# A gated cross-attention stack: weighing three scoring steps behind, with five buffers of exponentials

## The reference

```python
def attend(xn, ctx, l):                 # heads: 16 of 8 features (l = 0, 1, 3), 4 query heads of 32 with 1 key head (l = 2)
    q, k, v = heads(xn @ Wq), heads(ctx @ Wk), heads(ctx @ Wv)
    s = q @ k.T * scale                 # l = 0: + adj, masked; l = 1: rotary, causal; l = 2: rotary, masked by key
    return (softmax(s) @ v) @ Wo
x = x + tanh(g_xattn[0]) * attend(layernorm(x), ctx, 0)
x = x + tanh(g_ffn[0]) * route8(layernorm(x))            # the one of 8 matrices with the highest score, per token
x = x + tanh(g_xattn[1]) * attend(layernorm(x), ctx, 1)
x = x + tanh(g_ffn[1]) * top2_lora(layernorm(x))         # top 2 of 8 low-rank experts, relu
x = x + tanh(g_xattn[2]) * attend(layernorm(x), ctx, 2)
x = x + tanh(g_ffn[2]) * route8_gelu(layernorm(x))       # one of 8 experts of width 512, gelu, layer norm
x = x + tanh(g_xattn[3]) * attend(layernorm(x), ctx, 3)
x = x + tanh(g_ffn[3]) * moe(layernorm(x))               # not zero for the first two rows only
```

## Time and profile before

| what | us |
|---|---|
| median of three runs | 1077.09 |
| the profiled execution | 1068.41 |
| its span, first to last instruction | 1066.7 |
| PE busy | 880.5 |
| DVE busy | 787.8 |
| ACT busy | 493.7 |
| POOL busy | 302.4 |

### The profile page before, as it was taken

One profiled execution on the slowest core, in us unless ns is written; L12 is line 12 of the kernel. 1 busy time (PEld: TensorE's weight loads), 2 busy tenths in 40 slices (PEclk: granted clock), 3 DMA queues, 4 the chain that ended last, 5 costly groups with the idle time before them and its releaser, 6 DMA issues.

```text
span 1066.7 us, 19274 instructions
## 1 busy us (share of the span) xinstructions
PE 880.5 (83%) x7316; PEld 573.0 (54%) x7316; DVE 787.8 (74%) x1849; ACT 493.7 (46%) x753; POOL 302.4 (28%) x324
## 2 busy tenths in 40 slices
PE   1778787788899998887898877787888999998686
PEld 1533346454566676663465323564456667776443
DVE  3899998778666945449778999878779574554783
ACT  2655453345534532217874656234554343322475
POOL 3600246443443211100323023655335330110000
PEclk9999777698989999988999989677998999988899
DMA  9100000000000000000110000000000000000000
GB/s 322 33 2 2 2 1 1 1 2 2 2 1 2 2 1 6 6 1 2 42 32 21 2 2 1 1 1 2 3 3 1 1 2 1 1 1 1 2 7 17
DMA packets 11741, 14.26 MB, mean 13 GB/s; under 512 B 1604, under 2 KB 10716, under 8 KB 11396
## 3 DMA queue, kind: packets, MB, share of 16 engines
q1 hardware_dynamic: 11552, 12.88, 3.7%
q10 hardware_dynamic: 100, 0.14, 0.1%
HBM read 11.55 MB, written 1.05 MB: 12 GB/s over the span
## 4 chain that ended last, share of the span: by engine, by line
PE 43%; DVE 40%; ACT 7%; issue 6%; SPq 1%; DMA 1%; POOL 1%; DVEq 0%; ACTq 0%
PE banks L986 36%; DVE nm_row L1440 13%; DVE probs L1459 5%; PE pv L986 4%; ACT probs L943 2%; DVE qf_row L1470 2%; DVE wide L1529 2%; DVE st_row L1283 2%; PE banks L682 2%; DVE xn_row L1395 1%; DVE mv_row L1285 1%; DMA xn_row<-in_ctx 1%; ACT wide L965 1%; ACT qT_row L860 1%; ACT kT_row L860 1%
## 5 line engine op out<-in xcount | busy, mean ns | idle before, releaser
L1440 DVE TENSOR_REDUCE nm_row<-banks 128x4 f32<-128x1024 f32 (+1 forms) x192 | 210.3, 1128 | 39.2 <-PE banks L986 38.6
L776 POOL TENSOR_TENSOR rstd_row<-rstd_row,neghalf 128x2 f32<-128x2 f32 x66 | 47.6, 721 | 365.8 <-DVE rstd_row L1390 277.8
L943 ACT ACTIVATE probs<-banks 128x1024 f32<-128x1024 f32 (+1 forms) x144 | 128.2, 933 | 36.5 <-PE banks L986 35.9
L986 PE MATMUL banks<-wide,c 128*128 128x256 f32 x512 | 127.9, 406 | 0.0
L986 PE MATMUL banks<-qT_row,kT_row 50*128 50x256 bf16 (+2 forms) x896 | 89.9, 298 | 29.6 <-DVE nm_row L1440 15.6
L986 PE MATMUL pv<-probs,vpad 128*32 128x256 f32 (+1 forms) x1536 | 105.7, 395 | 9.8 <-ACT probs L938 6.6
L986 PE MATMUL banks<-kT_row,qT_row 48*128 48x256 bf16 (+2 forms) x896 | 92.3, 294 | 25.7 <-DVE nm_row L1440 15.7
L986 PEld LDWEIGHTS banks<-wide,c 128*128 128x128 f32 x512 | 101.0, 202 | 18.3 <-issue 0.9
L938 ACT ACTIVATE probs<-probs 128x1024 f32<-128x1024 f32 x64 | 67.5, 1056 | 50.0 <-DVE probs L1459 48.1
L986 PE MATMUL banks<-c,wide 128*128 128x128 f32 x512 | 85.4, 336 | 3.7 <-POOL wide L834 3.7
L986 PEld LDWEIGHTS banks<-c,wide 128*128 128x128 f32 x512 | 79.6, 245 | 8.1 <-issue 6.4
(11 more groups left out here) (220 smaller groups left out, 1585.5 us busy)
## 6 DMA issues: line engine op xcount, KB each, us to landing
c<-in_c SPq DMA_DIRECT2D x1, 2500.0 KB
wide<-in_mask SPq DMA_DIRECT2D x8, 256.0 KB, 2.9
qT_row<-mT_row SPq DMA_DIRECT2D x96, 4.0 KB
c<-in_c SPq DMA_DIRECT2D x1, 1194.5 KB
xn_row<-in_ctx SPq DMA_DIRECT2D x8, 128.0 KB, 3.5
x_row<-in_x SPq DMA_DIRECT2D x8, 128.0 KB, 2.4
late<-in_late SPq DMA_DIRECT2D x2, 512.0 KB, 15.4
out<-x_row SPq DMA_DIRECT2D x8, 128.0 KB, 2.0
```

The costliest lines, as they stand in the source:

```text
L776: return pool.tensor_tensor(t, t, neghalf[:, 0:n], ALU.pow)
L943: act.activation(dst[:, :, 0:w], src[:, :, 0:w], ACT.Exp, scale=1.0 if l == 2 else HD ** -0.5).then_inc(sem["probs"], 1)
L986: return pe.matmul(dst, lhsT, rhs, start=start, stop=stop, **kw)
L1440: V.tensor_reduce(nm[b][:, t, :, 2 * jp:2 * jp + 2], ps[:, :, :, 0:kn], AX.X, ALU.max, negate=True).then_inc(sem["max"], 1)
```

## The change

`AHEAD`, the number of scorings by which weighing stands behind in a row's list, goes from 2 to 3, and the ring `probs` from four buffers to five. The computation and the number of instructions are the same.

```diff
-STACKS, WIDES, PROBS, BANKS = 3, 2, 4, 7
+STACKS, WIDES, PROBS, BANKS = 3, 2, 5, 7
 COLS = 32
...
         for p in range(pairs + AHEAD):
             out += [("attend", l, row, p)] if p < pairs else []
             out += [("weigh", l, row, (p - AHEAD) // 2)] if p >= AHEAD and (p - AHEAD) % 2 else []
         out += [("divide", l, row), ("o_flip", l, row), ("mix", l, row)]
...
-AHEAD = 2
+AHEAD = 3
 LEAD = [280.3, 290.2, 324.8, 314.7, 4.7, -4.1, 22.7, 13.6]
```

## The result

The changed kernel takes 1099.77 us (median, 1095.51 to 1104.3) against 1077.09 us (1071.6 to 1081.12) for the kernel before in the same comparison: a ratio of 1.022, 95% interval [1.0174, 1.0265]. It is 22.7 us slower. The prediction said 1072 us and its range ended at 1091.

The account below looks back on a forecast made before the run. No engine alone was the bound: VectorE in layer 0, TensorE from 215 to 340 us, a chain of waits last. Terms -3.4 - 1.4 + 0 + 0 + 0 = -4.8 us, scaled to the median, gave 1072 us; range 1059 to 1091.

Parts of the forecast that it names:

- the exchange of w0 and s4, w1 and s6: In 24 wide turns two weighings go behind scorings, whose scores reach ScalarE earlier: -3.4 us, ends 0 and 18 gained.
- a rival that takes a gain back: Scorings wait for PSUM banks anyway, 25.8 us in all, so earlier ones only wait earlier: 1077 us, chance 0.18.
- ScalarE's waits for scores: Sign of being right: ScalarE's idle time before exponentials falls from 35.9 us to 20 to 30.
- The one rival that spoke of the clock: Row 1's routing lies open at 165 to 215 us and the clock stays low: 1091 us, chance 0.24.
- TensorE's waits before weighings: One more scoring covers each exponential that an exchanged weighing waits for: -1.4 us, 10.2 us of waits falling to 7 to 9.
- Layer 0: VectorE is full in layer 0's turns, so order does not count: 0, ends 6.0 us gained and 9.7 lost.
- The fifth buffer: One more buffer of exponentials, by itself worth 0 to 0.4 us; taken as 0.
- The reason beside it: With four buffers s4 would wait for w0 behind it, so the program could not be written in this order.
- What the planner moves along: Steps moved in layer 0's routed part: 0, ends 3.5 us gained for row 3 and 5 lost at row 1's routing.
- the place that I read: Layer 0's routed part: row 3's 3.48 us wait for `wide` goes, a new 1 to 5 us wait at row 1's one-hot.
- The last stretch: The kernel's end, where no engine is full and steps wait for each other: shorter by 1 to 2 us.
- The range of 1067 to 1077: The sum's own range for the whole kernel, with the buffers' and the tail's terms alone varied.

Follow-up runs that it names:

- swap_again: Kernel before with five buffers; on TensorE alone, first two weighings of each turn in layers 0, 1, 3 put behind a later scoring: 1100.06 us, ratio 1.0196.
- ring_only: Kernel before with a fifth buffer of exponentials and nothing else, every engine's order unchanged: 1079.03 us, ratio 0.9996.
- swap_layer3: Kernel before with five buffers and the exchange on TensorE's list in layer 3's eight turns alone: 1087.49 us, ratio 1.0115.
- swap_layer0: Kernel before with five buffers and the exchange on TensorE's list in layer 0's eight turns alone: 1073.19 us, ratio 0.9939.
- swap_layers03: Kernel before with five buffers and the exchange on TensorE's list in layers 0 and 3: 1082.03 us, ratio 1.0094.
- swap_only: The same kernel as swap_again, in an earlier comparison with four runs: 1098.71 us, too few and too scattered for a ratio.
- swap_layers13: Kernel before with five buffers and the exchange on TensorE's list in the sixteen turns of layers 1 and 3: 1088.6 us, ratio 1.0089.

## Why the prediction was wrong

**The step that failed** is the first: the exchange of w0 and s4, w1 and s6, priced at -3.4 us with ends 0 and -18. By itself, on the old lists, it costs 2.0%, some 21 us (swap_again). Three things were wrong in it, and a fourth point stays open.
- Its ends left out a loss. I gave each scoring a place one weighing earlier, and did not ask what the weighing had stood in front of. w0 gave ScalarE time to free the banks for the next scoring. Without it there, TensorE waits in front of s4 and s6, and a turn of layer 3 goes from 12.35 to 13.75 us at one and the same clock (ring_only, swap_layer3). The sum of scorings' bank waits was in front of me and served only for a rival that takes a gain back.
- ScalarE's waits for scores were to fall from 35.9 us to 20 to 30. They are 48.2 us, and 51.7 in swap_again; the old order has 35.9 and 40.5.
- The sum had no term for the clock. Most of the difference between the executions is longer matmuls. The one rival that spoke of the clock put its fall between 166 and 215 us, where it rose, and behind it, where 0.87 was measured, but 0.86 in ring_only's execution of the old order too. What fell was the clock of layer 3's turns, 0.89 in place of 1.00 from 500 to 580 us.
- The mechanism of the first point is shown in the old lists. In the kernel after, whose lists were planned anew, ScalarE waits longer and TensorE works longer, but its waits for banks that exponentials free are 12.6 us and were 12.7. How its 22.7 us divide is not shown.

**TensorE's waits before weighings**, -1.4 us, 7 to 9 us left: the way was right. By the two rows that made up the 10.2 us they fell further, to 4.8; with GpSimd's it is 7.5. In the old lists this was of no worth, since waits before scorings took their place (17.5 us for exponentials in swap_again, 11.8 in ring_only, 12.7 before).

**Layer 0** at 0, ends -6.0 and +9.7: alone it gave -0.6%, 6.6 us, just past its end. Where in the trace these 6.6 us lie I can't say: swap_layer0's profiled span, 1071.3 us, is between the two of the old order. With layer 1 exchanged as well the gain is gone.

**The fifth buffer** at 0: right (0.9996). The reason beside it was wrong. With four buffers TensorE could still run s4 ahead of w0, since a scoring's matmuls need only PSUM; s4's exponential would wait. The planner makes its lists for three behind with four buffers, too, and puts them 1.5 us above those with five by its own costs. The trace of before could not show this wait, and it was not run.

**What the planner moves along** at 0, ends -3.5 and +5: right as a sum with the exchange in place (0.2% between swap_again and after), and for the place that I read the signs came, 3.48 us down to 0.84 and 4.56 us new. Without the exchange the same moves cost 2.8%, so it is not a term that can be added.

**The last stretch** was to be 1 to 2 us shorter. The last turn, from copy to copy of `pv`, is 9.8 us in place of 10.1, and the turn two before it 14.8 in place of 13.8. The range of 1067 to 1077 us that the sum gave for itself does not follow from it either: with the terms named there at their ends it is 1069 to 1074.

**The scale.** I took the profiled execution as the kernel and scaled to the median. ring_only shows one order with a clock of 0.902 and of 0.878; a rise or fall of 0.024 goes with 20 us here. A change that shifts the clock by as much, as swap_again does by the medians of the runs (0.865 against 0.889), can move more than all terms of my sum.

**What stays open.** What of the kernel after's own loss is the exchange's, and why all three layers cost more than their parts. The clock of layer 3 bears some of it in the single executions shown. Layers 0 and 1 together, 1.2% above their sum at a clock of 1.00 in that stretch, have another cause, which I have not found; part of it may be the one chip on which they were compared.

## What to carry to other kernels

Before an instruction is moved ahead of another, ask what the one that now comes later was covering. A ready weighing ahead of a scoring that needs a bank was no delay but filled the wait: behind the scoring, it left TensorE idle for 0.73 and 0.66 us in one turn.

Where a planner makes the order from fitted numbers, compare a change at several settings of them, and make the exchange alone by position, too. Here leads moved by at most 1 us were worth 4.4%, more than the change, and a part that gained 0.6% by position lost 0.8% when planned.

Split the span into TensorE's busy time and the rest before explaining a difference: the kernels that lost by the clock and those that lost by waits tell themselves apart in one subtraction. Take more than one execution of the old order for it. Here two gave 186.2 and 181.4 us, and single turns of the same steps compared better than fixed stretches of time.

## What the runs showed of the hardware

One and the same order ran with a granted clock of 0.902 and 0.878 on average, 1066.7 and 1086.6 us of span. Before's runs went from 1066.91 to 1089.55 us over the five comparisons; the fastest had a clock of 0.901, the slowest 0.873. On the chip of the slowest alone, 26 runs went from 1072.15 to 1089.55 us.

Sixteen matmuls of a weighing take 1.07 us at 2.4 GHz and 1.93 us at 1.2 GHz, a factor of 1.80 and not 2. The same turn with the same order on TensorE took 13.75, 15.15 and 17.5 us at granted clocks of 1.00, 0.89 and 0.71 (swap_layer3; swap_layers03 and swap_only; swap_layers13 and swap_again), with TensorE idle for 2.7 to 2.8 us each time. Its busy share rose from 0.79 to 0.84 while the turn became 28% longer, so the busy share does not show the fall of the clock.
